# Layer norms of a 16-head attention: twelve of sixteen tiles moved from VectorE to ScalarE at both ends, and filling products placed elsewhere

## What is computed

```python
x = x + tanh(g_xattn[0]) * L0_xattn(layernorm(x), ctx)   # attn0, linear attention
x = x + tanh(g_ffn[0])   * L0_ffn(layernorm(x))          # ffn0, 8 experts, top 1
x = x + tanh(g_xattn[1]) * L1_xattn(layernorm(x), ctx)   # attn1, 16 heads over 64 keys
x = x + tanh(g_ffn[1])   * L1_ffn(layernorm(x))          # ffn1, 8 dense gated experts
x = x + tanh(g_xattn[2]) * L2_xattn(layernorm(x), ctx)   # attn2, one head
x = x + tanh(g_ffn[2])   * L2_ffn(layernorm(x))          # ffn2, 8 experts, top 1
x = x + tanh(g_xattn[3]) * L3_xattn(layernorm(x), ctx)   # attn3, 16 heads over 64 keys
x = x + tanh(g_ffn[3])   * L3_ffn(layernorm(x))          # ffn3, 8 experts, top 2
# layernorm: (x - mean) / sqrt(var + 1e-5) over the 256 numbers of a token
```

## Time and profile before

| | us |
|---|---|
| median of 3 runs | 2005.31 |
| lowest, highest | 2003.15, 2005.36 |
| the profiled execution, its own time | 2014.25 |
| its span, first to last instruction | 2012.5 |
| start of attn1, ffn0's last output copy to the first product behind the fillers | 339.6 to 374.8 |
| attn1's last values to ffn1's first product behind its fillers | 447.2 to 468.4 |
| attn3's last values to the router's logits of ffn3 | 1809.2 to 1825.1 |

### The profile page before, as it was taken

The page is one execution under the profiler, slowest core; times in us unless marked ns, Lnnn a source line. Parts: engine busy times, 40 slices in busy tenths (PEclk is TensorE's granted clock), DMA queues, the critical chain, the costliest instruction groups (busy, mean ns, idle before and its releaser), DMA issues.

```text
span 2012.5 us, 35094 instructions
## 1 busy us (share of the span) xinstructions
PE 1871.3 (93%) x11630; PEld 1575.0 (78%) x11630; DVE 1421.3 (71%) x2404; ACT 1083.3 (54%) x1979; POOL 712.3 (35%) x735
## 2 busy tenths in 40 slices
PE   7989997898999999999999999999988997897993
PEld 4669997786888888888888888888766997686993
DVE  4867776768777777777777777777766664766674
ACT  4347775565555555555555555555424664573771
POOL 3013432364443543534434435434002232352231
PEclk8999999999999999999999999999989999899997
DMA  4056663101100000000000000021104441203544
GB/s 124 1 156 182 200 184 97 31 2 32 32 16 31 31 16 31 16 31 31 16 31 31 16 31 31 16 97 62 38 32 147 143 144 45 75 2 114 167 144 139
DMA packets 113579, 138.96 MB, mean 69 GB/s; under 512 B 15332, under 2 KB 101606, under 8 KB 113504
## 3 DMA queue, kind: packets, MB, share of 16 engines
q1 hardware_dynamic: 105952, 121.70, 19.9%
q0 software_dynamic: 7552, 16.24, 2.7%
HBM read 117.22 MB, written 24.90 MB: 71 GB/s over the span
## 4 chain that ended last, share of the span: by engine, by line
PE 79%; DVE 10%; ACT 4%; issue 3%; DMA 2%; another core or an unknown queue 1%; ACTq 0%; SPq 0%; DVEq 0%; POOL 0%; POOLq 0%
PE ps L677 43%; PE ps L936 10%; PE ps L937 10%; PE ps L938 10%; PE ps L684 2%; PE ps L872 1%; ACT ps L1565 1%; DVE xs L1770 1%; DVE bn L1683 1%; ACT wsplit L1526 1%; DVE lnx L1672 1%; PE ps L1136 1%; PE ps L1095 1%; DVE h_lo L2120 1%
## 5 line engine op out<-in xcount | busy, mean ns | idle before, releaser
L677 PE MATMUL ps<-h_hi,wsplit 128*128 128x512 f32 (+3 forms) x2016 | 589.4, 350 | 1.8 <-DVE xT L1906 1.3
L677 PEld LDWEIGHTS ps<-h_hi,wsplit 128*128 128x128 f32 x2016 | 367.2, 188 | 48.4 <-DVE xT L1906 1.7
L677 PE MATMUL ps<-h_lo,wsplit 128*128 128x512 f32 (+3 forms) x1008 | 352.4, 350 | 0.0
L563 POOL TENSOR_TENSOR wsplit<-wraw,zero 128x256 fp32r<-128x256 f32 (+2 forms) x160 | 151.1, 960 | 501.0 <-PE ps L938 411.3
L1447 ACT ACTIVATE lnx<-ps 128x512 f32<-128x512 f32 x384 | 228.9, 597 | 107.3 <-PE ps L938 63.6
L677 PE MATMUL ps<-xTh,wsplit 128*128 128x256 f32 (+2 forms) x992 | 256.3, 312 | 20.9 <-DVE h_lo L2120 16.9
L1906 DVE TENSOR_TENSOR xT<-xT,ps 128x1024 f32<-128x1024 f32 x124 | 151.5, 1222 | 121.8 <-PE ps L677 121.8
L1456 ACT ACTIVATE h_act<-h_act 128x512 f32<-128x512 f32 x192 | 120.9, 629 | 207.9 <-DVE h_act L1884 207.8
L1460 ACT ACTIVATE h_hi<-ps 128x512 fp32r<-128x512 f32 x256 | 152.8, 597 | 146.3 <-PE ps L677 145.1
L2120 DVE TENSOR_TENSOR h_lo<-ps,h_hi 128x256 fp32r<-128x256 f32 (+2 forms) x248 | 117.7, 474 | 159.2 <-ACT h_hi L1569 152.3
L1893 DVE TENSOR_TENSOR ps<-h_act,ps 128x512 f32<-128x512 f32 x256 | 177.5, 694 | 45.0 <-PE ps L938 30.9
(11 more groups left out here) (289 smaller groups left out, 3634.1 us busy)
## 6 DMA issues: line engine op xcount, KB each, us to landing
wraw<-in_L_w SPq DMA_DIRECT2D x124, 512.0 KB, 3.6
wraw<-in_L_ffn_Wg SPq DMA_DIRECT2D x32, 256.0 KB, 2.8
wraw<-in_L_ffn_Wu SPq DMA_DIRECT2D x32, 256.0 KB, 3.0
wraw<-in_L_ffn_Wd SPq DMA_DIRECT2D x32, 256.0 KB, 3.6
x_tok<-lnx SPq DMA_DIRECT2D x12, 512.0 KB, 3.8
lnx<-y_tok SPq DMA_DIRECT2D x12, 512.0 KB, 6.3
y_tok<-lnx SPq DMA_DIRECT2D x3, 2048.0 KB, 13.9
wat<-in_attn SPq DMA_DIRECT2D x16, 256.0 KB, 4.9
```

Of the source, the lines that this page charges most:

```text
L563: return pool.tensor_tensor(out_, in_, zero[:, :].to_broadcast(shape), ALU.add)
L677: return pe.matmul(out_, lhsT, rhs, start=start, stop=stop)
```

## The change

A tensor `nmr` (minus mean times `st_rstd`, one number per token) and a semaphore `nmr_done` are new. VectorE makes it for groups 0 to 2 in `shift`; ScalarE then makes `lnx` of the twelve tiles of these groups as Identity(`xs` x `st_rstd` + `nmr`) in `norm_tiles`. VectorE keeps group 3. This is done at the beginning of attn1 and attn3 (norm `n`), and at their end for the feed-forward behind them (norm `n + 1`), so that `norm(n)` disappears from ffn1 and ffn3.

```diff
+            def norm_tiles(k, a, b):
+                for i in range(a, b):
+                    act.wait_ge(nmr_done, (NG - 1) * k + i // GROUP + 1)
+                    act.activation(lnx[:, i, :], xs[:, i, :], ACT.Identity, bias=nmr[:, i:i + 1], scale=st_rstd[:, i:i + 1]).then_inc(ln_done, 1)
...
+            def shift(n, g):
+                four = slice(g * GROUP, (g + 1) * GROUP)
+                dve.wait_ge(std_done, norm_no(n, g) + 1)
+                dve.scalar_tensor_tensor(out=nmr[:, four], in0=mv[:, four, 0], scalar=-1.0, in1=st_rstd[:, four],
+                                         op0=ALU.mult, op1=ALU.mult).then_inc(nmr_done, 1)
```

On VectorE (`add_rows` and `mha`; in `add_rows` the name `n` is the stage before, so its `n + 1` is the attention):

```diff
                     if i > 0:
                         next_stats(n, i - 1)
+                    if m is not None and g > 0 and i % GROUP == 0:
+                        norm_moments(n + 1, g - 1)
+                    if m is not None and g > 0 and i % GROUP == 2:
+                        shift(n + 1, g - 1)
...
                 for g in range(NG):
-                    add_rows(layer - 1, n - 1, g)
-                    if g > 0:
-                        norm_moments(n, g - 1)
+                    add_rows(layer - 1, n - 1, g, m)
                 next_stats(n - 1, NT - 1)
                 norm_moments(n, NG - 1)
-                norm(n)
                 bounds_of_mask()
-                for j in range(2):
-                    bound(j, j)
-                    maxima(j, j)
+                dve.wait_ge(ln_done, NT * n + 3 * GROUP)
+                norm_group(n, NG - 1)
+                bound(0, 0)
+                maxima(0, 0)
+                bound(1, 1)
+                maxima(1, 1)
                 step(0, 0, first=True)
...
+                for g in range(NG - 1):
+                    norm_moments(n + 1, g)
                 step(NT - 3, 1)
+                for g in range(NG - 1):
+                    shift(n + 1, g)
                 step(NT - 2, 0, ahead=False)
                 step(NT - 1, 1, ahead=False)
-                for g in range(NG - 1):
-                    norm_moments(n + 1, g)
                 residual(NT - 1)
                 next_stats(n, NT - 1)
                 norm_moments(n + 1, NG - 1)
+                dve.wait_ge(ln_done, NT * (n + 1) + 3 * GROUP)
+                norm_group(n + 1, NG - 1)
```

On ScalarE (`mha`, then the beginning of ffn2 and ffn3):

```diff
-                step(NT - 3, 1)
-                step(NT - 2, 0, queries=False)
-                step(NT - 1, 1, queries=False, more=False)
+                step(NT - 3, 1, rstds=True)
+                step(NT - 2, 0, queries=False, norms=(0, 2))
+                step(NT - 1, 1, queries=False, more=False, norms=(2, 6))
+                norm_tiles(2 * m + 1, 6, 3 * GROUP)
...
-                    if layer == 3:
-                        for g in range(NG - 1):
-                            norm_rstd(n, g)
                     weights_upper(0, 0, 0)
+                    weights_upper(0, 0, 1)
                     norm_rstd(n, NG - 1)
-                    for q in range(1, 4):
-                        weights_upper(0, 0, q)
...
                     copy_logits(layer, n, NG - 1)
+                    for q in range(2, 4):
+                        weights_upper(0, 0, q)
```

On PE (`mha`):

```diff
-                pe.wait_ge(x_done, NT * n - 4)
-                fill(0, 30)
+                pe.wait_ge(x_done, NT * (n - 1) + GROUP)
+                fill(0, 14)
...
                 pe.wait_ge(xt_done, NG * n + 1)
+                fill(0, 8)
+                turn_group(n, 1)
+                fill(0, 6)
                 query(0, True)
+                scores(0, True)
                 turn_group(n, 2)
-                scores(0, True)
...
                 output(NT - 1)
-                fill(0, 26)
```

29 lines of the change are left out of this document (19 added, 10 removed).

## The result

| | before | after |
|---|---|---|
| median, us | 2005.48 (15 runs, 2002.74 to 2009.25) | 2010.79 (15 runs, 2007.37 to 2013.63) |
| ratio after to before | | 1.0023, 95% interval 1.0015 to 1.0031 |
| the profiled execution's span, us | 2012.5 | 2011.0 |

The changed kernel is slower by 0.23%, 4.6 us (3.0 to 6.2); forecast were 3.9. The spans of the two profiled executions stand the other way round by 1.5 us, so they cannot be subtracted; stretches between the same two instructions must be compared. Some of these repeat closely: two profiles of the kernel before agree within 0.02 us at the starts of both attentions, in ffn1 and at attn3's end. Others do not: the same two profiles differ by 9.4 us ahead of attn1's first added tile, by 6.2 us between ffn1 and attn3, and by 3.5 us behind ffn3's routing.

What follows compares the result with a forecast made beforehand. PE, busy for 93% of the span, was taken to pace the kernel. Two attention starts +7.4, attn1's end -3.0 and attn3's end -0.5 gave +3.9 on the median 2005.31, so 2009.2 us; range 2003 to 2015.

Steps and rivals of the forecast that it cites:

- A tile on ScalarE: Norm tiles moved to ScalarE: 0.60 us for one, 0.50 from one to the next, against VectorE's 0.33.
- Case D: Rival: ScalarE's norm tile costs only 0.33 and the clock is up; -5.2 us together, 2000; chance 0.12.
- Start: Start of attn1 and attn3: early transposes gain nothing, second scores end 3.7 us later each; +7.4 for both.
- First query no earlier: Sign at attn1's start: first query product ends no earlier relative to the first added tile, despite transposes five us earlier.
- T: End of the second scores at an attention's start, 371.37 before; forecast 375.1 in attn1, 3.7 us later.
- From the start of `bound` to T are 3.9 us as before: Attention start: the stretch from `bound` to the second scores' end was taken as unchanged, 3.9 us.
- Case B: Rival: PE's clock falls again between first query and second scores, slowing the 32 fillers; +8.9, 2014; chance 0.21.
- Case C: Rival, no change: PE at the high clock early in the start and at the end; about -0.8, 2004.5; chance 0.17.
- End of attn1: Attn1's end into ffn1: differences start 4.3 us earlier, part lost to PE's low clock; -3.0 taken.
- End of attn3: Attn3's end into ffn3: ScalarE's copy and router logits 0.7 us earlier; -0.5 taken, bounds -2.0 and +1.5.
- PE waits 2.8 us for the copy, unfilled, and may slow down: Attn3's end: counterweight to the 0.7 us earlier copy, PE idle for 2.8 us and perhaps slower.
- ffn2: Two weight pieces moved behind ScalarE's copies in ffn2: nothing, at most 0.2 us.

Runs made afterwards that it cites:

- start_only: Changed kernel with the old end put back, so only the start of both attentions is changed; ratio to before 1.0034.
- two_groups: Changed kernel with the third group's norm at the start of both attentions back on VectorE; ratio to before 0.9990.
- start_filled: Changed kernel with 10 fillers ahead of the third group's transposes and 14 ahead of the fourth's at the start; ratio to before 1.0017.
- bound_first: Changed kernel with one edit: VectorE makes the first bound and maxima ahead of its norm group; one run, 2009.26 us.
- query_first: Changed kernel with start lists reordered: first bound ahead of VectorE's norm group, second query and scores ahead of the last eight transposes; ratio to before 1.0011.
- end_filled: end_only plus 30 fillers ahead of ffn1's last eight transposes and 22 ahead of ffn3's first logits; ratio to before 0.9957.
- end_only: Changed kernel with the old start of both attentions put back, so only the ends are changed; ratio to before 0.9972.
- before_again: Kernel before, without an edit, for a second profile; 1235.5 us from ffn1's first product to attn3's first added tile.
- early_query2: end_filled with a reordered start: early first query, ScalarE normalising groups 0 and 1, VectorE groups 2 and 3 between bound and maxima; ratio to before 0.9914.

## Why the prediction was right, point by point

**Direction and size.** +3.9 was forecast, +4.6 (3.0 to 6.2) measured, inside the range. The direction rests on a mechanism that the runs bear out: the starts lose more than attn1's end gains. The closeness of the size is in part luck, because errors cancelled. Against the stretches of after, the starts were put 1.0 too low together, attn3's end 1.8 and its pipeline 0.4 too low, attn1's end 0.6 too high, and -2.1 us in ffn1 were not in it at all. By other executions the misses have other sizes: with attn3's end at its average of 0 (below) that miss is 0.5 and not 1.8, and the starts of start_only, with the same code, are 1.2 longer together than those of after.

**A tile on ScalarE.** 0.60 and 0.50 were forecast from the pair in attn0; four take 2.07 and six 3.04, so 0.50 from one to the next and 0.59 for the last. Right. Case D, which hung on 0.33, falls.

**Start.** "First query no earlier": forecast 0.25 us earlier, measured 0.7 in attn1 and 0.5 in attn3; in attn1 the clock rose at 362.38, ahead of the query. From its end to T 9.5 were forecast, 10.4 measured. The chain to `bound` was right (query's end to `bound` 5.5, forecast 5.6), and two_groups confirms its largest link: without ScalarE's third group it is 3.4, shorter by the 2.06 us of that group. The step that failed is "From the start of `bound` to T are 3.9 us as before": it was 4.9, since the last transposes, released by the same norm tiles, stand ahead of the second query in TensorE's list and fell into the low clock. With the clock up it is 3.9, in two_groups and in start_filled. The clock so carries 0.7 to 1.0 of the 4 us of a start; bound_first shows that moving `bound` ahead of the norm group gains nothing. Of the bounds 2.9 to 4.6 for one start, three of four measured starts (4.0, 4.4, 4.6) keep inside, start_only's attn1 (5.0) does not. A small slip: 365.5 + 9.5 is 375.0, not 375.1.

**Case B, the clock falls again.** It did, at 369.2 in attn1 and at 1727.7 in attn3, but it rose before the 32 fillers, which took 3.67 us as before. The case was priced at 2.5 us in each attention, on the fillers; its price, 0.7 to 1.0, fell on the transposes and the query ahead of them. In bound_first and in attn3 of query_first it did reach the fillers, which took 5.5, 5.0 and 5.2 us. "No pause here exceeds 3 us" was no protection: the pauses were 1.2 and 1.8 us.

**Case C.** Its -0.8 does not come out of its terms: +2.0 for both starts, -4.1 and the -0.5 of attn3 make -2.6, and the +2.0 lies below the prediction's own lower bound of 2.9 for one start. The measured +4.6 (3.0 to 6.2) leaves the case out.

**End of attn1.** -3.0 was forecast (bounds -2.1 to -4.1), -3.94 and +0.37 of P measured, -3.6. The differences came 4.7 earlier behind the last `ot` where 4.85 (4.3 and 0.55) were forecast, so 7.9 behind it; the "about 9" among the signs to look for did not follow from the prediction's own working, which gives 7.75. The clock was down for 3.4 us, not for the whole stretch, and took 0.6 (end_filled against end_only). Where it was down for 6.8 us, in query_first and start_filled, E1 won only 2.9 and 3.2; the bounds -2.1 to -4.1 hold all six kernels with this end, and -2.9 to -4.1 is what they show. The four tiles ahead of the last `inverse` cost 0.37, forecast 0.55. ScalarE's tiles were not held by GpSimd: six took 3.04 us beside it in attn1 and 3.04 without it in attn3. The Trainium skill (SBUF — State Buffer, SBUF: two separate sides) had it so, and the trace agrees; VectorE's tiles were held (4.28 us beside GpSimd against 1.38 without).

**End of attn3.** -0.5 was forecast, +1.28 measured in after. The copy came earlier by 1.4, twice the 0.7 forecast. The step that failed is "PE waits 2.8 us for the copy, unfilled, and may slow down": it was named and then not priced. PE waited 2.93 us and the clock was down for 6.8. By the table of six kernels this wait costs 0, 1.5 or 2.7 us by how long the clock is down, and the end as a whole -1.4 to +1.3, 0.0 on average. The bounds -2.0 and +1.5 were right; the sign in after says little about the next execution.

**ffn2.** Forecast nothing. From ffn1's last transposes to attn3's first added tile after took 243.5 us, start_only with the old order 240.4, before 245.8 and before_again 239.7: the spread of executions hides anything of this size.

**What was missing.** The new tensor and semaphore were taken for free. Declaring them was worth -2.1 us. Without it the changed kernel would be about 6.5 us slower by the stretches, still inside the range.

## What to carry to other kernels

Before moving work to an idle engine, look for a gap in that engine's list ahead of the consumer, since the early result may gain nothing without one: here the first transposes came 6.7 us early, and the next group's norm, the copy and the fillers behind it gave back all but 0.7, and the rest of the chain turned 0.7 us ahead into 4.0 behind. Walk every list from the first early result to the first late consumer, and ask of each wait that is taken away what else stands ahead of the consumer on its own engine, and which third engine (here GpSimd) it lets loose. And compare kernels by stretches between the same two instructions, with the ends of a stage, the stage itself and untouched stages apart: it shows where the time goes, which medians cannot. But one profile is enough only where the clock keeps still in the stretch; where it moves, the same code varied by 2.7 us here, and several profiles are needed.

## What the runs showed that I had not expected

- An unused tensor of 64 bytes a partition, allocated ahead of others, and declared together with an unused semaphore, made 995.85 us of ffn1 take 993.71, with the same instructions, repeatable within 0.02 us over three executions without it and within 0.16 over eleven with it. Whether it is the tensor's place, which buffer's, and why, stays open. Whoever adds or removes a tensor should allow for some 0.1% of the kernel's time and look for it in an untouched stage.
- Releasing GpSimd early cost VectorE's norm tiles: four took 2.96 us instead of 1.38. The maxima of early_query2, which ran beside GpSimd from 367.27 on, kept their 1.22 us.
- TensorE's clock fell behind pauses of 1.2 and 1.8 us with work in between (3.55 of the 6.83 us ahead of the fall busy), and at attn3's end a piece of code of 12.5 us took up to 15.2, in step with how long the clock was down. Where it falls differs between executions of one kernel (E1 of before and before_again).
- Best of all kernels run here: early_query2, 0.9914 of before; one of its parts, end_filled, has 0.9957.
